# GpSimd's causal gate matrices by affine selection, and the output scaling moved ahead of the expert gathers

## What is computed

```python
# attention branch: gated delta rule, 16 key heads, 32 value heads, 128 x 128 states
q, k, v, z = split(xn @ w_qkvz)                   # then a causal convolution of 4 taps and silu on q, k, v
g = -exp(A_log) * softplus(a + dt_bias)           # decay of each head and token; beta = sigmoid(b)
for t in tokens:                                  # per sequence and head
    state = state * exp(g[t])
    delta = (v[t] - state.T @ k[t]) * beta[t]
    state = state + outer(k[t], delta)
    o[t] = state.T @ q[t]
xg = o * silu(z)
y = xg * rsqrt(mean(xg * xg) + 1e-6) * norm_w     # the scaling of the gated output
attention = y @ w_out
# expert branch: 64 of 2048 experts for each token, found by product keys
h = silu(xn @ W_up.T + b_up) @ W_down.T + b_down
z = dot(h, down_embed[indices])                   # 64 gathered rows of 128
experts = sum(silu(z * softmax(scores)) * up_embed[indices])   # 64 gathered rows of 256
```

## Time and profile before

| | before |
|---|---|
| median of 3 runs | 3445.3 us (3440.46 to 3448.35) |
| the profiled execution | 3440.7 us, span 3438.8 us |
| VectorE busy | 3012.3 us, 88% |
| TensorE busy | 2992.4 us, 87% |
| GpSimd busy | 2306.0 us, 67% |
| ScalarE busy | 1794.2 us, 52% |
| granted TensorE clock, mean | 0.953 of full speed |

### The profile page before, as it was taken

How to read it: one execution, slowest core, us unless ns; L and a number is a source line. 1 busy time by engine, 2 the same in 40 slices (tenths; PEclk the granted TensorE clock), 3 DMA queues, 4 the chain that set the end, 5 groups by cost and what they waited for, 6 DMA issues and landing times.

```text
span 3438.8 us, 56504 instructions
## 1 busy us (share of the span) xinstructions
PE 2992.4 (87%) x18444; PEld 2451.1 (71%) x18444; DVE 3012.3 (88%) x9101; ACT 1794.2 (52%) x4111; POOL 2306.0 (67%) x2650
## 2 busy tenths in 40 slices
PE   7844999989998989899989988898989899998997
PEld 4422777778776777677767777777777777777776
DVE  5996999989998999899989898998899898989996
ACT  3322555555554555455545555555555555555553
POOL 0005777777767776777778777877777667877764
PEclk9976999999999999999999999999999999999999
DMA  1003545544555545454545554544555454544553
GB/s 60 1 1 104 137 132 141 135 131 132 137 139 135 131 133 139 130 133 133 141 126 138 134 138 124 149 127 134 138 138 137 125 139 132 146 129 135 144 132 89
DMA packets 541827, 427.98 MB, mean 124 GB/s; under 512 B 247008, under 2 KB 450784, under 8 KB 541536
## 3 DMA queue, kind: packets, MB, share of 16 engines
q1 hardware_dynamic: 476000, 222.98, 24.0%
q0 software_dynamic: 65536, 201.39, 22.0%
HBM read 345.61 MB, written 45.09 MB: 114 GB/s over the span
## 4 chain that ended last, share of the span: by engine, by line
DVE 36%; POOL 35%; PE 14%; issue 9%; DMA 5%; ACT 1%; SPq 0%; DVEq 0%; POOLq 0%; ACTq 0%
POOL rows L952 22%; DVE rows L1193 9%; POOL xg L931 9%; DVE qkv L1177 6%; DVE mix L1210 4%; POOL rms L928 3%; DVE E L1165 3%; DMA rows<-table,pick 3%; PE ps L579 3%; PE ps L500 3%; PE ps L517 2%; PE ps L665 1%; DVE topi L1024 1%; DVE xg L1147 1%; PE ps L521 1%
## 5 line engine op out<-in xcount | busy, mean ns | idle before, releaser
L952 POOL DMA_INDIRECT rows<-table,pick x1024 | 1157.2, 1130 | 326.3 <-issue 326.3
L551 PE MATMUL ps<-X,AT 128*128 128x128 f32 x3072 | 417.7, 294 | 119.2 <-DMA XT<-whole 119.2
L551 PEld LDWEIGHTS ps<-X,AT 128*128 128x128 f32 x3072 | 392.9, 207 | 169.8 <-DMA XT<-whole 167.3
L806 ACT ACTIVATE qkv<-qkv 128x512 f32<-128x512 f32 x256 | 161.5, 631 | 518.6 <-DVE qkv L1177 518.6
L571 PE MATMUL ps<-XT,E 128*128 128x128 f32 x3072 | 400.6, 277 | 0.0
L801 ACT ACTIVATE raw<-ps 128x512 f32<-128x512 f32 x256 | 152.8, 597 | 433.2 <-PE ps L517 433.2
L1210 DVE SCALAR_TENSOR_TENSOR mix<-rows,zc,mix 128x256 f32<-128x256 f32 x896 | 375.1, 476 | 0.0
L571 PEld LDWEIGHTS ps<-XT,E 128*128 128x128 f32 x3072 | 368.9, 192 | 0.0
L939 POOL TENSOR_SCALAR gm<-cst,gn 128x128 f32<-128x128 f32 x512 | 362.9, 723 | 6.7
L1193 DVE CUSTOM_DVE_ANT_0 rows<-rows,h2c 128x128 f32<-128x128 f32 x1024 | 342.9, 399 | 9.2 <-SPq L328 4.7
L931 POOL TENSOR_SCALAR xg<-xg,rms 128x128 f32<-128x128 f32 x520 | 324.9, 637 | 7.0
(11 more groups left out here) (167 smaller groups left out, 6333.4 us busy)
## 6 DMA issues: line engine op xcount, KB each, us to landing
Wvz<-wvz SPq DMA_DIRECT2D x64, 512.0 KB, 3.3
xb<-xnT SPq DMA_DIRECT2D x64, 512.0 KB, 4.4
whole<-AT SPq DMA_DIRECT2D x128, 256.0 KB, 3.6
X<-whole SPq DMA_DIRECT2D x128, 256.0 KB, 3.9
XT<-whole SPq DMA_DIRECT2D x128, 256.0 KB, 4.4
wo<-woh SPq DMA_DIRECT2D x65, 256.0 KB, 4.4
Wkq<-wkq SPq DMA_DIRECT2D x64, 256.0 KB, 2.5
rows<-table,pick POOLq DMA_INDIRECT x1024
```

Of the source, the lines that this page charges most:

```text
L551: done = mm(ps[:, g, (a % 4) * P:(a % 4 + 1) * P], AT_b[:, a, :], src[:, a, :], start=True, stop=True)
L952: pool.indirect_dma_start(rows[:, m, :], None, table[:, :], bass.IndirectOffsetOnAxis(ap=pick[:, m:m + 1], axis=0)).then_inc(gathered, 16)
```

## The change

Three edits.

1. In `gate_sums` the eight products become two `affine_select` instructions. Each takes four columns of `gn`, spread over 128 positions, and writes 128 x 512 of `gm`: the value where `j - p >= 0`, zero elsewhere. That is the same matrix. `gm_p` counts 2 in a pass instead of 8.
2. `finish()` moves from between the two halves of the gathers to a place ahead of the wait for `e_v` and of `pick`, so that all 16 gathers come after it.
3. The copy of `h2c` now counts a new semaphore `h2c_p`, and VectorE waits for it in front of the dots.

```diff
-                    pe.wait_ge(sm["gm_p"], at("gm_p", 8))
+                    pe.wait_ge(sm["gm_p"], at("gm_p", 2))
...
+            zero = pool.to_reg(0.0)
+
...
                 pool.wait_ge(sm["gn_p"], at("gn_p", calls))
-                for a in range(TASKS):
-                    pool.tensor_scalar(gm[:, a, :], mask(C_LE), gn[:, a:a + 1], None, ALU.mult).then_inc(sm["gm_p"], 1)
+                for g in range(2):
+                    pool.affine_select(gm[:, 4 * g:4 * g + 4, :], gn[:, 4 * g:4 * g + 4].unsqueeze(2).broadcast_to([P, 4, P]),
+                                       [[0, 4], [1, P]], ALU.is_ge, zero, base=0, channel_multiplier=-1).then_inc(sm["gm_p"], 1)
...
                 if n is not None:
+                    finish()
                     pool.wait_ge(sm["e_v"], at("e_v", 3))
                 picks(f)
-                pool.tensor_copy(h2c[:, :], h2_all[:, bass.ds(f // 4, 1), :].rearrange("p a c -> p (a c)"))
+                pool.tensor_copy(h2c[:, :], h2_all[:, bass.ds(f // 4, 1), :].rearrange("p a c -> p (a c)")).then_inc(sm["h2c_p"], 1)
                 gather(0)
                 if n is not None:
-                    finish()
                     pool.wait_ge(sm["mix_v"], at("mix_v", 1))
                 gather(K // 2)
...
                     dve.wait_ge(gathered, 256 * n + 256)
+                    if place["u"]:
+                        dve.wait_ge(sm["h2c_p"], last("h2c_p"))
                     for k in range(16):
                         expert_dot(k)
```

More of the change, by code:

```diff
@@ L145, in program @@
                  "km_v kq_v ssk_v s_v at_v e_v conv_v ys0_v r1_v ys1_v xg_v acc_v rms_v elim_v dot_v "
-                 "gn_p gm_p cols_p pick_p norm_p mt_p rms_p y_p zero_p scal_step silu_e sim_v mix_v "
+                 "h2c_p gn_p gm_p cols_p pick_p norm_p mt_p rms_p y_p zero_p scal_step silu_e sim_v mix_v "
                  "h2_s gate_v gate_s").split()
@@ L172, in program @@
                    s_v=1, at_v=2, rms_v=1, mix_v=1, elim_v=1, ys0_v=2, ys1_v=2, r1_v=4, acc_v=2, cols_p=1, zero_p=1,
-                   gn_p=1, gm_p=8, rms_p=1, y_p=8, pick_p=1, norm_p=1, mt_p=2, w_vz=32, xb_in=16, wo_in=16, w_kq=32,
+                   h2c_p=1, gn_p=1, gm_p=2, rms_p=1, y_p=8, pick_p=1, norm_p=1, mt_p=2, w_vz=32, xb_in=16, wo_in=16, w_kq=32,
                    blocks_out=32, blocks_in=16, inv_out=32, inv_in=64)
```

## The result

The changed kernel takes 3839.2 us in the median of 4 runs (3836.2 to 3845.5), the kernel before 3446.8 beside it: ratio 1.114, 95% interval 1.111 to 1.117. In a later series on another chip it took 3838.3, ratio 1.113 (1.110 to 1.116). The forecast was 3807, range 3720 to 3935. The profiled execution took 3836.8 us, span 3835.0.

The account below looks back on a forecast made before the run. It took VectorE's work and GpSimd's gathers as almost level at 47.4 us a pass; the new loop summed to 53.7. 390.6 + 63 x 53.7 + 36 (stalls) - 3 (first build) gave 3807 us, range 3720 to 3935.

Parts of the forecast that it names:

- the new wait: In front of VectorE's dots (L1196): VectorE waits for `gathered`, some 6 to 8 us a pass, 5 to 8 in the profile.
- Two signs: Profile checks: L1150 should not idle for TensorE; `rms` much later than 20 us after the first dot would refute the forecast.
- the first or the second rival: First: TensorE at half clock, 3870 to 4000 us, chance 0.18. Second: selections hold VectorE, about 3920 us, chance 0.13.
- first dot's end to `rms`: VectorE's stretch from the first dot's end to the start of `rms`, taken unchanged from one pass: 18.94 us.
- sixteen gathers: GpSimd's 16 gathers in a row: 22.0 us a pass, between bounds of 19.8 and 23.0.
- last gather to the end of the next first dot: From the last gather's end to the end of the next `gn` copy, landing included: 4.84 us.
- the first build: Gate matrix built ahead of pass 0, with TensorE's first differences waiting for it: some 3 us saved once.
- The selections at zero: GpSimd's two selections beside VectorE's dots: 0 us taken; the rival said 1 to 2.5 us a pass more, chance 0.13.
- the coupling: VectorE's first dot is held until GpSimd's run `MT`, `cols`, `xr`, `gn` is over, so it ends with `gn`.
- Half clock: Rival: TensorE's level transforms run at 1.2 GHz, `rms` comes 1 to 3 us later, 3870 to 4000 us; chance 0.18.
- Gathers at their floor: Rival: the block of sixteen gathers takes 19.8 us instead of 22.0, 51.5 a pass, 3668 us; chance 0.12.
- gathers covered: Rival: not slower, a pass is VectorE's own 45.4 to 45.5 us, 3290 us in all; chance 0.02.

Follow-up runs that it names:

- third experiment: Changed kernel with VectorE's mean squares ahead of the triangular matrices: 4095.5 us in a disturbed series, 3634.6 us (ratio 1.0536 to the kernel before) when repeated.
- second experiment: Kernel before with only the scaling moved ahead of the gathers, eight products kept: 3791.3 us (ratio 1.088), repeated at 3800.3 us (1.1035).
- fourth experiment: Kernel before, with GpSimd waiting for its own `MT` before it copies `cols`: 3501.4 us, ratio 1.004.
- second series: Later set of four runs on another chip, with the changed kernel run again as it is: 3838.3 us, ratio 1.113 to the kernel before.
- fifth experiment: Changed kernel plus unread 512-column TensorE products: fifteen a pass 4193.4 us (ratio 1.216 to the kernel before), seven a pass 3850.3 us (1.118).
- sixth: Changed kernel with `pick` and six gathers after the first taps, then the scaling, then ten gathers: 3392.8 us, ratio 0.985 to the kernel before.

## Why the prediction came out as it did

**The bound before, and the new wait: right in the main.** The changed kernel's new bound is VectorE's wait for the gathers, 7.6 to 7.8 us in an ordinary pass where 5 to 8 was forecast; GpSimd's idle stands in front of the power with 18.2 us (12 to 17 forecast; the two selections take only 1.3 us, and `rms` is a microsecond late); one block of 22.2 us stands between `h2c` and `norm`. Putting the scaling behind nothing but `rms` costs the pass because `rms` is late on VectorE, and nothing in the change moved it. The third experiment shows that lever directly. Two signs came out otherwise. L1150 still waits for TensorE, 0.72 us in this pass and 47.7 us in all (197.5 before), where none was forecast. And `rms` starts 21.4 us after the first dot does, in place of 20.6; by the prediction's own list that points to the first or the second rival, and both have a part in it.

**The sum.** By term, forecast and pass at 1587.85:

| term | forecast | measured |
|---|---|---|
| first dot's end to `rms` | 18.94 | 19.98 |
| `rms` to power | 0.24 | 0.24 |
| power to first gather | 7.70 | 7.59 |
| sixteen gathers | 22.0 | 22.22 |
| last gather to the end of the next first dot | 4.84 | 4.32 |
| loop | 53.7 | 54.35 |

The mean over the 63 passes is 54.7 ((3778.36 - 331.64) / 63, the first and the last first dot), and 390.0 lie outside, where 390.6 less 3 was put. The first dot of pass 0 starts anywhere between 331 and 341 us in the profiles of these kernels, so the 3 us of the first build cannot be read. Of the 30 us by which the forecast was too low, nearly all is the loop.

The mis-sized term is the first, which I carried over unchanged. Two things are in it. The other fifteen dots take 4.27 us instead of 3.53. With the products kept (the repeat of the second experiment) they take 3.71: so 0.56 us come with the selections, which I put at nothing, and 0.18 a third dot that is now held beside `xr`, since the first is let go earlier. And VectorE waits 0.60 and 0.20 us at the level products and 0.20 at `km` for TensorE, where it waited only the last 0.20 in the pass before; the rest of the stretch is shorter. That is TensorE's half clock (below).

That the term came within 1.04 us is partly luck. The 18.94 us of my pass are the fourth longest of 63: the median in the kernel before is 18.23, and half of the 0.7 above it is a later `QS`, behind TensorE's slow group of 3.61 us. From the median the same sum gives 53.0 us a pass and some 3763 us, 74 too low instead of 30, though still inside the range.

**The selections at zero: wrong.** I argued that GpSimd's products and scalings read SBUF too and leave their neighbours on VectorE their usual duration. For the products that holds roughly: with them a dot now and then takes 0.36 us instead of 0.28. A selection of 128x512 (0.66 us) beside a dot holds it for 0.43 to 0.47 us, once for each.
The Trainium skill (SBUF — State Buffer, Who interferes with whom) has a VectorE instruction with two SBUF inputs and a GpSimd instruction that reads SBUF exclude each other for a whole instruction. The dots beside the selections agree, at somewhat less than the selection's length; the dots beside the products do not, since they lose about 0.08 us against products of 0.72.
The rival said 1 to 2.5 us a pass, at `MT`'s rate. Measured are 0.45: passes of equal clock take 54.35 us in the changed kernel and 53.90 in the second experiment's repeat at half clock, 53.15 and 52.69 at full. That is below the rival's range; a selection takes 0.66 us, half of `MT`'s, and a dot beside it loses less than that.

**The end of the first dot: the coupling was looser than read.** It ends 0.65 us ahead of the end of `gn` in most passes of the changed kernel, with the copy of `cols`, while in the kernel before it ended with `gn` itself. That gave back 0.52 us of the 4.84. The fourth experiment shows that a gap of 0.06 us in GpSimd's stream is enough to let VectorE in. Why the run breaks there without a pause that the trace shows, once the dots start during `MT` after a long wait, is open.

**Half clock: the rival's mechanism is there, at 1.2 us a pass.** TensorE dips as the rival said, twice a pass, and the mean clock falls by 0.05. What the dip at the levels costs, the changed kernel's own passes show. In 5 of the 62 behind pass 0 the level products run at full clock. Here is one of them by its first dot and `rms`, and then the stretch from TensorE's first level product (L564) to VectorE's third (L1168), in that pass and in the pass shown above (busy of PE, PEld, DVE, ACT and POOL, then PEclk, DMA share and GB/s):

```profile
1041.09 1.26 DVE L1196 CUSTOM_DVE_ANT_0 rows<-rows,h2c 128x128 f32<-128x128 f32 x1 [7.96 <-DMA rows<-table,pick]
...
1061.13 0.17 DVE L1138 TENSOR_SCALAR rms<-sumsq 128x8 f32<-128x8 f32 x1
```

```profile
1049.14:1054.85 5.71, 5.62 (x48) 5.43 (x48) 5.64 (x12) 2.43 (x5) 0.00 (x0) 1.00 0.00 0
1596.02:1602.42 6.40, 6.40 (x42) 6.40 (x43) 5.73 (x13) 2.95 (x6) 0.00 (x0) 0.73 0.01 3
```

In both passes TensorE starts its level products 0.74 us after VectorE's first one starts. The stretch then takes 5.71 us at a granted clock of 1.00 and 6.40 at 0.73. At full clock VectorE waits for none of these products and `rms` follows the first dot's end by 18.78 us; at 0.73 it waits 0.60 and 0.20, and `rms` follows after 19.98. The other fifteen dots take 4.27 us in both. No run changed this clock alone, but the passes sort by it. Among those of this execution without a stalled gather and with 4.27 us of dots the loop lasts 53.15 us at 1.00 in this stretch (5 passes), 54.2 at 0.75, 54.35 at 0.73 (most of them) and 54.9 at 0.66. The second series's profile of the same kernel gives the same figures, with 7 passes at full clock. So half clock at the levels costs 1.2 us in nine passes of ten, an estimate of some 70 us in all, more than the selections. I had priced it at 2 us a pass, gave it 0.18, and left it out of the sum; the slow pass that I took my first term from made up for 0.7 of the 1.2. In the kernel before the levels run at full clock in every one of these passes. The fifth experiment raised the clock only in front of the other hole, where TensorE is not waited for. A dip costs where the engine behind it is being waited for, and only there.

**Gathers at their floor; gathers covered.** Neither came: the block is 22.2 us in nearly every pass, with its slow ones (1.25 to 1.74 us) in the middle beside VectorE's wide products and taps, and not 19.8. The stalls of single gathers came again as taken (332.8 us of idle in all, 326.3 before).

## What to carry to other kernels

Before moving work ahead of a queue of transfers, ask for the latest input that the moved work waits for: everything behind it inherits that wait. Here the mirror image paid: transfers whose buffers are free go first, and the waiting step goes in among them at the point where its input arrives. A shorter instruction sequence on an engine that idles anyway is worth nothing, while its wider instructions can still hold up those of another engine that run beside them. And take the terms of such a sum from the median pass, not from the one that you happened to read: here a slow pass hid 0.7 us.

## What the runs showed of the hardware

- A GpSimd selection of 128x512 takes 0.66 us and costs the VectorE dot beside it 0.43 to 0.47; eight products of 128x128 at 0.72 us each cost the dots beside them about 0.08 each. Fewer instructions disturbed more.
- A first dot held by GpSimd's back-to-back instructions is let in by a pause of 0.06 us; in the changed kernel it was let in without one.
- With the four loads of `X` and `XT` (1 MB) issued 1.3 or 3.9 us before the last gather ends, its rows are there 4.2 and 4.7 us after it ended (medians of the sixth and third experiment); with the loads issued 7.6 us before, 2.8 us.
- With TensorE's granted clock at 0.73 in the stretch of the levels VectorE reaches `rms` 1.20 us later than at 1.00, in passes of one and the same execution.
- In one series, and on the same chip not in a later one, readers of TensorE's results were released late while gathers were being issued, in the pass shown 7.6 us after its group had ended. It lifted the kernel before by 1.3% and one variant by 13% (4095 against 3635 us). A ratio from such a series misleads even with the reference beside it: the variants differ in how much of this they catch. What it is stays open.
